# Layer 1's probabilities: transposed by VectorE and a DMA round trip in place of TensorE, with attention one slot later

## The chip, the cores and the metric

The kernel runs on one core of a Trainium2 chip. The core has TensorE (matrix products and transposes, into the eight banks of PSUM), VectorE, ScalarE, GpSimd and SyncE, which here only starts DMA transfers. In profile rows they are PE (PEld is its weight load), DVE, ACT, POOL and SP. Each engine runs its own instructions in order and waits for others through semaphores. The metric is the device time in microseconds. The kernel before takes 1692.25 us, the median of 3 runs (1692.12 to 1692.57).

## The reference, cut to what matters

Two layers, each a cross-attention and a feed-forward, are added to `x` (8 batches of 128 tokens, 512 wide). The change is in the attention of layer 1. It has 8 groups (one per key/value head), each of 4 query heads; queries and keys are normalised before the scores. Keys and values come from 128 context tokens and from the 128 tokens themselves, so a row has 256 keys.

```python
kv = jnp.concatenate([context, latents], axis=1)
q = rms_norm((latents @ Wq)...)          # 32 heads of 128
k = rms_norm((kv @ Wk)...)               # 8 heads of 128
v = (kv @ Wv)...
scores = jnp.einsum('bhgqd,bhkd->bhgqk', qg, k) * scale
probs = jax.nn.softmax(scores.astype(jnp.float32), axis=-1)
out = jnp.einsum('bhgqk,bhkd->bhgqd', probs, v)
return out @ Wo                          # 4096 -> 512
```

## The kernel before

Every product is made of three passes: each fp32 operand is split in a high part (rounded to fp32r) and a low part (the rest), and high x high, low x high and high x low are added in PSUM. ScalarE mostly makes the high parts and VectorE the low parts (`*_hi`, `*_lo`).

Layer 1 is 64 **slots**, 8 groups `t` of 8 batches `j`; slot `i = 8t + j`. The order of work is written out by hand for each engine in its `slot1(t, j)`; groups 1 to 6 are a hardware loop. Slot `i` works on several stages of different batches at once (counts start at 1, so head `i` is the one whose scores were made in slot `i - 1`):

- TensorE (`slot1` at L2498): keys and values of `i + 2`, transposes of queries and keys of `i + 1` (L2514, L2519), the output projection of `i - 1`, the transposes of the probabilities of `i` (L2488, eight 128x128 ones), the queries of `i + 2`, the scores of `i + 1`, the attention output of `i`.
- ScalarE (L1222): four exponentials of `i` (L1204), high parts of transposed queries (L1230) and keys (L1232), of the values with the squares of the keys (`kv_out`, L1182 and L1183), of the transposed probabilities (L1215), copy and squares of the queries (L1189, L1190), the high part of the attention output (L1220).
- VectorE (L1936): two reciprocals of the sums (L1917), low parts of queries and keys (L1945, L1947), in slots 1 to 5 of a group the low part of a piece of the next group's weights (`split_lo`, L1865), the addition of the projected output to the residual (L1921), low parts of the values (L1875), mean square of the keys (L1870), in slots 0 to 4 the high part of a weight piece (`split_hi`, L1859), the low part of the transposed probabilities (L1927), scaling of the keys (L1882), mean square of the queries (L1889, L1891), the maxima of the scores (L1907) and the shift of the exponentials `nb` (L1912), the low part of the attention output (L1933).
- GpSimd (L741): multiplies the probabilities by the reciprocals in two halves (L748), and two small powers (L610).
- SyncE (L566): one load of keys and values of the context per slot (L554) and one of weights in slots 1 to 5 (L577).

Each PSUM bank of layer 1 has one use: queries `Q1B`, scores `S0B` and `S1B`, transposed probabilities `T0B` and `T1B`, attention output `O1B`, projection `Y1B`.

Of the kernel before, what the change touches and what calls it, by code (L numbers as in the profile page):

```python
# [57 lines left out]
def build(nc, x, ctx_t, mask, gates, wk0, wv0, wq0, w0, bias0, lnw, qweight, lut4, lut8, ffn0_bias, w1, qk_norm, ffn1_w, ffn1_bias, out):  # L58
    stack = ExitStack()
    with stack:  # L60
# [184 lines left out]
        def z_rows(phase_no, b):  # L245
# [123 lines left out]
        kv1d = nc.dram_tensor("keys_values_of_context_of_layer_1", (KV, P, B, 256), fp32, kind="Internal").ap()  # L369


        @block.sync
        def _(sp):
# [192 lines left out]
            def slot1(t, j):  # L566
# [32 lines left out]
        def _(pool):  # L599
# [141 lines left out]
            def slot1(t, j, tail=False):  # L741
# [3 lines left out]
                if not (first and j == 0):  # L745
                    for half_p, done in ((0, norm1_first), (2, norm1_second)):
# [3 lines left out]
                                           ALU.mult).then_inc(done, 1)  # L750
# [29 lines left out]
        def _(act):  # L780
# [419 lines left out]
            def exponentials1(count, parity):  # L1200
                act.wait_ge(shift1_done, count)
                wait(act, pt1_ps, count - 1)
                for a in range(4):
# [3 lines left out]
                    if a == 1:  # L1207
                        last_op.then_inc(exp1_first, 1)
                last_op.then_inc(exp1_done, 1)

            def probabilities_hi(count):
                act.wait_ge(pt1_ps, count)
                wait(act, o1_ps, count - 1)
                for kc, done in ((0, pt1_hi_first), (1, pt1_hi_second)):
                    nc.scalar.activation(pt_hi[:, kc, :], (T0B, T1B)[kc][:, :], ACT.Copy).then_inc(done, 1)  # L1215

            def output1_hi(count):
                act.wait_ge(o1_ps, count)
                wait(act, y1_ps, count - 1)
                nc.scalar.activation(ot1_hi[:, :], O1B[:, :], ACT.Copy).then_inc(ot1_hi_done, 1)  # L1220

            def slot1(t, j):  # L1222
# [19 lines left out]
                if not (first and j == 0):  # L1242
# [8 lines left out]
                if not (first and j == 0):  # L1251
# [27 lines left out]
        def _(dve):  # L1279
# [650 lines left out]

            def output1_lo(count):
                dve.wait_ge(ot1_hi_done, count)
                nc.vector.tensor_tensor(ot1_lo[:, :], O1B[:, :], ot1_hi[:, :].bitcast(fp32),  # L1933
                                        ALU.subtract).then_inc(ot1_lo_done, 1)

            def slot1(t, j):  # L1936
# [20 lines left out]
                if last and j in (3, 5, 7):  # L1957
# [682 lines left out]
```

## Time and profile before

| | |
|---|---|
| median of 3 runs | 1692.25 us (1692.12 to 1692.57) |
| span of the profiled execution | 1690.2 us, of which layer 1's slots are about the last 750; its own time is given as this span alone |
| TensorE busy | 1669.2 us, 99% |
| VectorE busy | 1190.2 us, 70% |
| ScalarE busy | 1001.1 us, 59% |
| GpSimd busy | 601.3 us, 36% |
| chain that ended last | TensorE 87%, VectorE 7%, ScalarE 3% |
| granted TensorE clock | nine tenths of full speed or more in all 40 slices |

The runs' times are some 2 us above the span, which is from the first to the last instruction. The busy time of an engine counts overlapping instructions once. The chain that ended last is followed back from the last instruction, at each step to what released it or to the instruction before on its engine. An idle time in brackets in a row of the timeline is the time that the engine stood just before that instruction, with what released it.

### The profile page before, as it was taken

The page shows a single profiled execution, that of the slowest core. Times are in us where ns is not written, and L with a number is a line of the kernel's source. Part 1 is how long each engine was busy: PE and PEld are TensorE (multiplying, and loading weights), DVE is VectorE, ACT ScalarE, POOL GpSimd, SP SyncE. Part 2 cuts the span into 40 slices and gives each one's busy share as a digit, 9 for nine tenths or more (in the row PEclk, how much of TensorE's full clock was granted, in tenths as well). Part 3 has the DMA queues.
Part 4 walks back from the last instruction along what each step waited for, and adds up shares of the span by engine and source line. Part 5 has one row for each costly group of instructions (what it writes and reads, how often), then busy time and mean ns, then how long its engine had stood idle before and what let it go on. Part 6 is the DMA issues. An engine that isn't in the chain of part 4 may idle for free.

```text
span 1690.2 us, 30970 instructions
## 1 busy us (share of the span) xinstructions
PE 1669.2 (99%) x10269; PEld 1480.7 (88%) x10269; DVE 1190.2 (70%) x2245; ACT 1001.1 (59%) x2540; POOL 601.3 (36%) x584
## 2 busy tenths in 40 slices
PE   9999999999999999999999999999999999999998
PEld 8999999999988888888888888888888888888887
DVE  6444437676787777777779776767686767777677
ACT  5444343345767677776776666566656665666663
POOL 3322223211433443534425533333333333333343
PEclk9999999999999999999999999999999999999999
DMA  6444444545233333333332110101010111111001
GB/s 236 176 161 149 149 169 153 193 138 179 77 108 100 110 111 99 124 99 109 111 104 96 35 51 26 63 22 50 25 62 22 50 37 49 35 37 40 14 7 50
DMA packets 80591, 153.31 MB, mean 91 GB/s; under 512 B 6544, under 2 KB 58128, under 8 KB 76944
## 3 DMA queue, kind: packets, MB, share of 16 engines
q1 hardware_dynamic: 80528, 152.50, 26.9%
q8 instruction: 36, 0.59, 0.1%
q14 instruction: 27, 0.22, 0.0%
HBM read 108.43 MB, written 44.04 MB: 90 GB/s over the span
## 4 chain that ended last, share of the span: by engine, by line
PE 87%; DVE 7%; ACT 3%; issue 2%; DMA 0%; POOL 0%; DVEq 0%; SPq 0%; ACTq 0%
PE bank L2091 21%; PE bank L2038 15%; PE bank L2040 15%; PE bank L2039 14%; PE bank L2268 6%; PE bank L2488 3%; PE bank L2226 2%; PE bank L2304 2%; PE bank L2388 2%; PE bank L2514 2%; DVE wl L1538 1%; PE bank L2214 1%; DVE sc L1546 1%; DVE residual L1553 1%; DVE residual L1555 1%
## 5 line engine op out<-in xcount | busy, mean ns | idle before, releaser
L2038 PE MATMUL bank<-w_hi,xt_hi 128*128 (+2 forms) x512 | 178.6, 349 | 0.8 <-DVE qt_lo L1945 0.8
L748 POOL TENSOR_TENSOR p<-p,rn 128x512 f32<-128x512 f32 x128 | 133.1, 1041 | 120.9 <-DVE rn L1917 117.8
L2040 PE MATMUL bank<-w_hi,xt_lo 128*128 (+2 forms) x512 | 173.1, 338 | 0.0
L2039 PE MATMUL bank<-w_lo,xt_hi 128*128 (+2 forms) x512 | 171.8, 336 | 0.0
L691 POOL TENSOR_TENSOR pr<-pr,rn 128x512 f32<-128x512 f32 x64 | 67.5, 1055 | 291.4 <-DVE rn L1563 291.4
L1204 ACT ACTIVATE p<-bank,nb,q_r 128x256 f32<-128x256 f32 x256 | 141.0, 561 | 4.4 <-DVE nb L1912 1.9
L610 POOL TENSOR_TENSOR q_r<-q_ms,half 128x4 f32<-128x4 f32 x64 | 64.4, 1007 | 193.7 <-DVE q_ms L1891 193.7
L1049 ACT ACTIVATE pr<-sc,nmax 128x128 f32<-128x128 f32 x256 | 99.9, 391 | 39.9 <-DVE nmax L1548 39.5
L2038 PE MATMUL bank<-w0o_hi,ot_hi 128*128 128x512 f32 x256 | 105.5, 412 | 5.0 <-DVE residual L1555 4.5
L610 POOL TENSOR_TENSOR k_r<-k_ms,half 128x2 f32<-128x2 f32 x64 | 56.9, 888 | 147.8 <-DVE k_ms L1870 147.8
L2038 PE MATMUL bank<-w_hi,ot_hi 128*128 (+1 forms) x256 | 106.1, 415 | 1.3 <-DVE ot_lo L1933 1.3
L2038 PEld LDWEIGHTS bank<-w_hi,xt_hi 128*128 128x128 f32 x512 | 96.6, 189 | 11.9 <-DVE qt_lo L1945 1.0
L2040 PEld LDWEIGHTS bank<-w_hi,xt_lo 128*128 128x128 f32 x512 | 96.4, 188 | 11.6
L2039 PEld LDWEIGHTS bank<-w_lo,xt_hi 128*128 128x128 f32 x512 | 96.7, 189 | 10.7
L2091 PE MATMUL bank<-vw_hi,t_hi 128*128 128x256 f32 x368 | 104.1, 283 | 0.6 <-DVE vw_lo L1327 0.6
L2091 PE MATMUL bank<-vw_hi,t_lo 128*128 128x256 f32 x368 | 104.1, 283 | 0.0
L2091 PE MATMUL bank<-vw_lo,t_hi 128*128 128x256 f32 x368 | 104.1, 283 | 0.0
L1220 ACT ACTIVATE ot_hi<-bank 128x512 fp32r<-128x512 f32 x64 | 38.3, 598 | 109.5 <-PE bank L2040 109.5
L1189 ACT ACTIVATE q_sb<-bank 128x512 f32<-128x512 f32 x64 | 38.2, 597 | 106.3 <-PE bank L2040 106.3
L2040 PE MATMUL bank<-w_hi,ot_lo 128*128 (+1 forms) x256 | 100.4, 392 | 0.0
L2040 PE MATMUL bank<-w0o_hi,ot_lo 128*128 128x512 f32 x256 | 100.1, 391 | 0.0
L2039 PE MATMUL bank<-w0o_lo,ot_hi 128*128 128x512 f32 x256 | 99.9, 390 | 0.0
(293 smaller groups left out, 5603.6 us busy)
## 6 DMA issues: line engine op xcount, KB each, us to landing
stage<-w SPq DMA_DIRECT2D x35, 512.0 KB, 3.3
keys_of_layer<-kout SPq DMA_DIRECT2D x16, 1024.0 KB, 4.8
values_of_layer<-vout SPq DMA_DIRECT2D x16, 1024.0 KB, 5.2
kt<-keys_of_layer SPq DMA_DIRECT2D x64, 256.0 KB, 3.4
vs<-values_of_layer SPq DMA_DIRECT2D x64, 256.0 KB, 2.8
vraw<-wv SPq DMA_DIRECT2D x10, 1024.0 KB, 6.8
kraw<-wk SPq DMA_DIRECT2D x16, 512.0 KB, 5.6
stage0o<-w SPq DMA_DIRECT2D x16, 512.0 KB, 3.2
```

The source lines that it names most:

```text
L610: pool.tensor_tensor(dst, src, exponent, ALU.pow).then_inc(done, 1)
L691: pool.tensor_tensor(by4(pr), by4(pr), rn[:, :].unsqueeze(2).to_broadcast([P, 4, P]), ALU.mult).then_inc(norm_done, 1)
L748: pool.tensor_tensor(p1[:, half_p:half_p + 2, :], p1[:, half_p:half_p + 2, :], rn1[:, half_p:half_p + 2].unsqueeze(2).to_broadcast([P, 2, ...
L1049: last_op = nc.scalar.activation(by4(pr)[:, a, :], by4(sc)[:, a, :], ACT.Exp, bias=nmax[:, a:a + 1], accum_out=ssum[:, a:a + 1])
L1204: last_op = nc.scalar.activation(p1[:, a, :], by2((S0B, S1B)[a // 2][:, :])[:, a % 2, :], ACT.Exp, bias=nb1[:, a:a + 1], scale=q_r[:, pari ...
L1220: nc.scalar.activation(ot1_hi[:, :], O1B[:, :], ACT.Copy).then_inc(ot1_hi_done, 1)
L2038: nc.tensor.matmul(out_ap, l_hi, r_hi, start=(c == 0), stop=False)
L2039: nc.tensor.matmul(out_ap, l_hi, r_lo, start=False, stop=False)
L2040: op = nc.tensor.matmul(out_ap, l_lo, r_hi, start=False, stop=(c == n - 1))
L2091: op = nc.tensor.matmul(out_ap, l, r, start=start, stop=False, skip_group_check=True)
L2268: op = nc.tensor.matmul(bank[which][:, :], l[:, a, c, :], r[:, c, :], start=start, stop=False, skip_group_check=True)
L2488: op = nc.tensor.transpose(by4((T0B, T1B)[kc][:, :])[:, a, :], p1[:, a, tok(kc)], ident[:, :])
```

## The change

For heads 1 to 60 TensorE no longer transposes the probabilities. VectorE transposes them in blocks of 32x32 (`probabilities_in_blocks`, two instructions of 128x512), SyncE writes the blocks to DRAM (512 KB, one DMA) and, once that has landed, reads them back with four DMAs that put each block where the full transpose has it (512 KB in all). ScalarE makes the high part and VectorE the low part from this copy in SBUF, one instruction of 1024 columns each in place of two of 512. The copy of head `i` is used in slot `i + 1`, so its attention output, projection and addition to the residual all come one slot later. For heads 61 to 64 TensorE transposes as before; slot 61 makes the attention output and projection of head 60 and the attention output of head 61. In the last group the row statistics and normalisations of the feed-forward that follows move by a slot.

```diff
+            pblk = place.enter_context(nc.sbuf_tensor("probabilities_in_blocks", [P, 1024], fp32))
+            ptr1 = place.enter_context(nc.sbuf_tensor("probabilities_transposed", [P, 2, 1024], fp32))
...
+        pbd = nc.dram_tensor("blocks_of_probabilities", (4, P, 1024), fp32, kind="Internal").ap()
+        LAGGED = U - 4
+        lagged = lambda t, j: not (isinstance(t, int) and t == TL - 1 and j >= LAGGED % BODY + 1)
+        in_blocks = lambda ap: ap.rearrange("p (kb kc a q) -> p a kc kb q", kb=4, kc=2, a=4)
+        by_key_block = lambda ap: ap.rearrange("p (qb kc n) -> p kc qb n", qb=4, kc=2)
...
 # SyncE, at the end of each slot, behind its two loads
+                if lagged(t, j) and not (static and t == 0 and j < 1):
+                    probabilities_round_trip(BODY * t + j, j % 4)
+            def probabilities_round_trip(count, place):
+                sp.wait_ge(blocks1_done, 2 * count)
+                sp.dma_start(pbd[place, :, :], pblk[:, :]).then_inc(blocks1_out, 16)
+                sp.wait_ge(blocks1_out, 16 * count)
+                for kb in range(4):
+                    sp.dma_start(ptr1[32 * kb:32 * (kb + 1), place % 2, :].rearrange("k (qb n) -> k qb n", qb=4),
+                                 pbd[place, :, 256 * kb:256 * (kb + 1)].rearrange("(qb k) n -> k qb n", qb=4)).then_inc(ptr1_in, 16)
...
 # ScalarE: behind the high part of the keys, ahead of kv_out
+            def moved_probabilities_hi(count, parity):
+                act.wait_ge(ptr1_in, 64 * count)
+                wait(act, o1_ps, count - 1)
+                nc.scalar.activation(pt_hi[:, :, :].rearrange("p kc (qb n) -> p kc qb n", qb=4), by_key_block(ptr1[:, parity, :]),
+                                     ACT.Copy).then_inc(pt1_hi_done, 1)
...
+                if (lagged(t, j) or i == LAGGED + 1) and not (first and j < 2):
+                    moved_probabilities_hi(i - 1, (j - 1) % 2)
...
 # VectorE
+            def moved_probabilities_lo(count, parity):
+                dve.wait_ge(pt1_hi_done, count)
+                nc.vector.tensor_tensor(pt_lo[:, :, :].rearrange("p kc (qb n) -> p kc qb n", qb=4), by_key_block(ptr1[:, parity, :]),
+                                        pt_hi[:, :, :].bitcast(fp32).rearrange("p kc (qb n) -> p kc qb n", qb=4),
+                                        ALU.subtract).then_inc(pt1_lo_done, 1)
+            def probabilities_in_blocks(count):
+                wait(dve, blocks1_out, 16 * (count - 1))
+                for half_p in (0, 2):
+                    dve.wait_ge(norm1_done, 2 * count - 1 + half_p // 2)
+                    nc.vector.transpose(in_blocks(pblk[:, :])[:, half_p:half_p + 2],
+                                        p1[:, half_p:half_p + 2, :].rearrange("p a (kc kb q) -> p a kc kb q", kc=2, kb=4)).then_inc(blocks1_done, 1)
...
+                if (lagged(t, j) or i == LAGGED + 1) and not (first and j < 3):
+                    accumulate1(i - 2, (j - 3) % B)
+                if not lagged(t, j) and i > LAGGED + 1:
                     accumulate1(i - 1, (j - 2) % B)
+                if lagged(t, j) and not (first and j < 1):
+                    probabilities_in_blocks(i)
...
+                if lagged(t, j) and not (first and j < 2):
+                    output1_lo(i - 1)
...
 # TensorE
-                if not (first and j < 2):
-                    output_projection1(i - 1, own if j >= 2 else other)
+                if (lagged(t, j) or i == LAGGED + 1) and not (first and j < 3):
+                    output_projection1(i - 2, own if j >= 3 else other)
...
-                if not (first and j < 1):
...
+                if not lagged(t, j):
+                    if i > LAGGED + 1:
+                        output_projection1(i - 1, own)
                     transposed_probabilities1(i)
...
+                if lagged(t, j) and not (first and j < 2):
...
+                    attention_output1(i - 1, (j - 2) % 4)
+                if not lagged(t, j):
+                    if i == LAGGED + 1:
+                        output_projection1(i - 1, own)
                     attention_output1(i, (j - 1) % 4)
```

The middle of a VectorE slot with both weight splits (`j` = 3, group 0), before. `residual` is the addition of the projection, `stage` the staged weights, and `fbias` here holds the scaled keys:

```order
L1947 SCALAR_TENSOR_TENSOR kt_lo<-bank,kw,kt_hi 128x256 [waits kt1_hi_done]
L1865 TENSOR_TENSOR w_lo<-stage,w_hi 128x1024 [waits w1_hi_2]
L1921 SCALAR_TENSOR_TENSOR residual<-bank,tg,residual 128x512 [waits y1_ps]
L1875 TENSOR_TENSOR v_lo<-keys_values_of_context,v_hi 128x128 [waits k1_squared]
L1875 TENSOR_TENSOR v_lo<-bank,v_hi 128x128
L1870 TENSOR_SCALAR k_ms<-k_ss 128x2 [waits k1_squared]
L1859 TENSOR_SCALAR w_hi<-stage 128x1024 [waits w1_in_3]
L1927 TENSOR_TENSOR pt_lo<-bank,pt_hi 128x512 [waits pt1_hi_first]
L1927 TENSOR_TENSOR pt_lo<-bank,pt_hi 128x512 [waits pt1_hi_second]
L1882 TENSOR_SCALAR fbias<-keys_values_of_context,k_r 128x128 [waits k1_root_done]
```

The same stretch of the same slot in the changed kernel:

```order
L2007 SCALAR_TENSOR_TENSOR kt_lo<-bank,kw,kt_hi 128x256 [waits kt1_hi_done]
L1907 TENSOR_TENSOR w_lo<-stage,w_hi 128x1024 [waits w1_hi_2]
L1963 SCALAR_TENSOR_TENSOR residual<-bank,tg,residual 128x512 [waits y1_ps]
L1984 STREAM_TRANSPOSE probabilities_in_blocks<-p 128x2x2x4x32 [waits norm1_done,blocks1_out]
L1984 STREAM_TRANSPOSE probabilities_in_blocks<-p 128x2x2x4x32 [waits norm1_done]
L1917 TENSOR_TENSOR v_lo<-keys_values_of_context,v_hi 128x128 [waits k1_squared]
L1917 TENSOR_TENSOR v_lo<-bank,v_hi 128x128
L1912 TENSOR_SCALAR k_ms<-k_ss 128x2 [waits k1_squared]
L1901 TENSOR_SCALAR w_hi<-stage 128x1024 [waits w1_in_3]
L1975 TENSOR_TENSOR pt_lo<-probabilities_transposed,pt_hi 128x1024 [waits pt1_hi_done]
L1924 TENSOR_SCALAR fbias<-keys_values_of_context,k_r 128x128 [waits k1_root_done]
```

Two transposes have come in ahead of the values' low parts, and the two low parts of the probabilities from PSUM have become one from SBUF at the same place.

TensorE between the output projection (`w_hi,ot_hi`) and the queries (`w_hi,xt_hi`), group 0, before:

```order
L2038 MATMUL bank<-w_hi,ot_hi 128x512
L2039 MATMUL bank<-w_lo,ot_hi 128x512
L2040 MATMUL bank<-w_hi,ot_lo 128x512
L2488 MATMUL bank<-ident,p 128x128 [waits norm1_first,pt1_lo_done]
L2488 MATMUL bank<-ident,p 128x128 x3
L2488 MATMUL bank<-ident,p 128x128 [waits norm1_second]
L2488 MATMUL bank<-ident,p 128x128 x3
L2038 MATMUL bank<-w_hi,xt_hi 128x512 [waits qt1_lo_done]
```

And in the changed kernel, same place:

```order
L2113 MATMUL bank<-w_hi,ot_hi 128x512
L2114 MATMUL bank<-w_lo,ot_hi 128x512
L2115 MATMUL bank<-w_hi,ot_lo 128x512
L2113 MATMUL bank<-w_hi,xt_hi 128x512 [waits qt1_lo_done]
L2114 MATMUL bank<-w_lo,xt_hi 128x512
```

The eight transposes are gone from between them.

## Rows read from the trace of the kernel before

**Rows 1.** The page's first part: busy time of each engine.
```profile
PE 1669.2 (99%) x10269; PEld 1480.7 (88%) x10269; DVE 1190.2 (70%) x2245; ACT 1001.1 (59%) x2540; POOL 601.3 (36%) x584
```

**Rows 2.** Busy time by window: slot 2 of group 5 (columns PE, PEld, DVE, ACT, POOL, clock, DMA).
```profile
1417.84:1429.12 11.28, 11.28 (x69) 9.96 (x69) 8.84 (x20) 6.94 (x22) 4.16 (x5) 1.00 0.16 58
```

**Rows 3.** TensorE's waits, 1010 to 1690 us: total, times, longest.
```profile
PE bank L2038 <- DVE ot_lo L1933: 1.3, 3, 0.8
```

**Rows 4.** The chain that ended last, 1485 to 1690 us: start, duration.
```profile
1498.15 0.87 PE bank L2488 x8
```

**Rows 5.** Timeline of VectorE, the same slot 2: start, duration, line, operation.
```profile
1417.84 0.69 DVE L1945 TENSOR_TENSOR qt_lo<-bank,qt_hi 128x512 fp32r<-128x512 f32 x1 [0.32 <-ACT qt_hi L1230]
...
1418.84 1.22 DVE L1865 TENSOR_TENSOR w_lo<-stage,w_hi 128x1024 f32 x1
1419.98 0.74 DVE L1921 SCALAR_TENSOR_TENSOR residual<-bank,tg,residual 128x512 f32<-128x512 f32 x1
...
1421.11 0.69 DVE L1859 TENSOR_SCALAR w_hi<-stage 128x1024 f32 x1
1421.71 1.28 DVE L1927 TENSOR_TENSOR pt_lo<-bank,pt_hi 128x512 fp32r<-128x512 f32 x2
1422.91 0.28 DVE L1882 TENSOR_SCALAR fbias<-keys_values_of_context,k_r 128x128 f32<-128x128 f32 x1
...
1423.99 0.69 DVE L1889 TENSOR_REDUCE q_ss<-q_sq 128x4 f32<-128x512 f32 x1 [0.55 <-ACT q_sq L1190]
...
1426.11 0.16 DVE L1912 TENSOR_TENSOR nb<-nmax,q_r 128x4 f32<-128x4 f32 x1
...
1429.12 0.69 DVE L1945 TENSOR_TENSOR qt_lo<-bank,qt_hi 128x512 fp32r<-128x512 f32 x1 [0.32 <-ACT qt_hi L1230]
```

**Rows 6.** Timeline of ScalarE, in and around the same slot.
```profile
1419.35 0.20 ACT L1183 ACTIVATION_READ_ACCUMULATOR fbias<-bank 128x1 f32 x1
1420.10 1.09 ACT L1215 ACTIVATE pt_hi<-bank 128x512 fp32r<-128x512 f32 x2 [0.55 <-PE bank L2488]
...
1426.31 0.56 ACT L1204 ACTIVATE p<-bank,nb,q_r 128x256 f32<-128x256 f32 x1
...
1428.49 0.60 ACT L1230 ACTIVATE qt_hi<-bank 128x512 fp32r<-128x512 f32 x1
...
1429.32 0.33 ACT L1182 ACTIVATE v_hi<-keys_values_of_context 128x128 fp32r<-128x128 f32 x1
```

**Rows 7.** Timeline of VectorE in slot 6, which has no weight split: all its waits.
```profile
1464.35 0.75 DVE L1921 SCALAR_TENSOR_TENSOR residual<-bank,tg,residual 128x512 f32<-128x512 f32 x1 [0.30 <-PE bank L2040]
...
1465.85 1.29 DVE L1927 TENSOR_TENSOR pt_lo<-bank,pt_hi 128x512 fp32r<-128x512 f32 x2 [0.28 <-ACT pt_hi L1215]
...
1469.11 0.69 DVE L1889 TENSOR_REDUCE q_ss<-q_sq 128x4 f32<-128x512 f32 x1 [1.52 <-ACT q_sq L1190]
```

**Rows 8.** Groups by line, 1194 to 1284 us: busy us, mean ns.
```profile
L1907 DVE TENSOR_REDUCE nmax<-bank 128x2 f32<-128x512 f32 x16 | 10.3, 686 | 0.0
...
L1859 DVE TENSOR_SCALAR w_hi<-stage 128x1024 f32 x5 | 3.4, 685 | 0.0
```

**Rows 9.** DMA issues, whole run: KB each, median us to landing.
```profile
stage<-w SPq DMA_DIRECT2D x35, 512.0 KB, 3.3
...
keys_values_of_context<-lues_of_context_of_layer SPq DMA_DIRECT2D x64, 128.0 KB, 2.4
...
lues_of_context_of_layer<-kout SPq DMA_DIRECT2D x8, 512.0 KB, 4.0
```

**Rows 10.** Timeline of TensorE: two matmuls of 512 columns in one product.
```profile
1405.45 0.39 PE L2040 MATMUL bank<-w_hi,ot_lo 128*128 x1
...
1405.68 0.40 PE L2038 MATMUL bank<-w_hi,ot_hi 128*128 x1
```

**Rows 11.** Timeline of TensorE, first group: its first wait for probabilities.
```profile
954.40 0.63 PE L2488 MATMUL bank<-ident,p 128*128 128x128 f32 x4 [2.18 <-POOL p L748]
```

**Rows 12.** Timeline of VectorE in the last group.
```profile
1611.78 1.29 DVE L1294 BATCH_NORM_STATS2 stats<-residual 128x6 f32<-128x512 f32 x2
```

More of the change, by code:

```diff
@@ L749, in slot1 @@
                                            rn1[:, half_p:half_p + 2].unsqueeze(2).to_broadcast([P, 2, 256]),
-                                           ALU.mult).then_inc(done, 1)
+                                           ALU.mult).then_inc(norm1_done, 1)
+                if last and j == 6:
+                    row_roots(3, 1)
                 if not tail and not (last and j == BODY - 1):
@@ L1201, in exponentials1 @@
                 act.wait_ge(shift1_done, count)
-                wait(act, pt1_ps, count - 1)
+                if isinstance(count, int) and count > LAGGED + 1:
+                    act.wait_ge(pt1_ps, count - 1 - LAGGED)
+                else:
+                    wait(act, blocks1_done, 2 * (count - 1))
                 for a in range(4):
@@ L1250, in slot1 @@
                     transposed_hi(2, 5)
-                if not (first and j == 0):
+                if (lagged(t, j) or i == LAGGED + 1) and not (first and j < 2):
+                    output1_hi(i - 1)
+                if not lagged(t, j):
+                    if i == LAGGED + 1:
+                        probabilities_hi(i)
                     output1_hi(i)
@@ L1956, in slot1 @@
                     transposed_lo(3, 0)
-                if last and j in (3, 5, 7):
-                    dve.wait_ge(acc1_done, i - 1)
-                    row_stats(3, (j - 3) // 2)
+                if last and j in (4, 7):
+                    dve.wait_ge(acc1_done, i - 2 if j == 4 else i - 1)
+                    row_stats(3, (4, 5, 7).index(j))
                 if last and j == 2:
@@ L1969, in slot1 @@
                     k_mean(i + 2)
+                if last and j in (5, 6):
+                    normed_rows(3, 2 * j - 10)
+                    normed_rows(3, 2 * j - 9)
                 if first and j == 0:
@@ L1979, in slot1 @@
                     split_hi(t + 1, j, (t + 1) % 2)
-                if lag1 and not (last and j == BODY - 1):
+                if (lagged(t, j) or i == LAGGED + 1) and not (first and j < 2):
+                    moved_probabilities_lo(i - 1, (j - 1) % 2)
+                if not lagged(t, j) and LAGGED + 1 < i < U - 1:
                     probabilities_lo(i)
@@ L1984, in slot1 @@
                     q_mean(i + 2)
+                if i == LAGGED + 1 if isinstance(i, int) else False:
+                    output1_lo(i - 1)
+                    probabilities_lo(i)
                 maxima1(i + 1, j % 2)
+                if last and i == LAGGED + 1:
+                    accumulate1(i - 1, (j - 2) % B)
+                    dve.wait_ge(acc1_done, i - 1)
+                    row_stats(3, 1)
                 if first and j == 0:
@@ L2527, in slot1 @@
                     transpose_rows(2, 5 + 2 * j)
-                if not (first and j < 1):
-                    if first and j == 1:
-                        pe.wait_ge(xt_lo_done, 3 * B - 2)
+                if not lagged(t, j):
+                    if i > LAGGED + 1:
+                        output_projection1(i - 1, own)
                     transposed_probabilities1(i)
@@ L2539, in slot1 @@
                     pe.wait_ge(facc_done, B)
+                if not lagged(t, j) and i == LAGGED + 1:
+                    attention_output1(i - 1, (j - 2) % 4)
                 pe.wait_ge(qt1_lo_done, i + 1)
                 pe.wait_ge(kt1_lo_done, i + 1)
-                wait(pe, exp1_done, i)
+                wait(pe, exp1_done, 2 * i)
                 for a in range(4):
@@ L2546, in slot1 @@
                 op.then_inc(s1_ps, 1)
[L2547 to L2548 removed]
+                if lagged(t, j) and not (first and j < 2):
+                    if first and j == 2:
                         pe.wait_ge(xt_lo_done, 3 * B)
+                    attention_output1(i - 1, (j - 2) % 4)
+                if not lagged(t, j):
+                    if i == LAGGED + 1:
+                        output_projection1(i - 1, own)
                     attention_output1(i, (j - 1) % 4)
```

78 lines of the change are left out of this document (41 added, 37 removed).

## The prediction

> **What bounds the kernel now.** I read the page first: TensorE is busy for 99% of the span, VectorE for 70% [rows 1]. A busy TensorE is not yet a bound one, so the waits came next: from 1010 us to the end TensorE waits for named work 1.3 us in three places [rows 3], and the chain that ended last runs through each slot's eight transposes as a piece of 0.87 us [rows 4]. In layer 1 the pace is TensorE's: 11.28 us a slot, in which VectorE is busy 8.84 us [rows 2]. Taking 0.87 us out of TensorE gives a pace of 10.41 us, if nothing else needs longer.
>
> VectorE's timeline says something else does. VectorE's work is a ring through ScalarE: it issues `nb`, ScalarE runs four exponentials and the high part of the queries, and only then can VectorE start `qt_lo`; all its other work but `ot_lo` and two reciprocals stands behind that. From `nb` at 1426.11 to the next `qt_lo` at 1429.12 are 3.01 us [rows 5], of which ScalarE is in the exponentials and the copy from 1426.31 on [rows 6]. Once around is 11.28 us (1417.84 to 1429.12), and the one real wait in it, outside those 3.01 us, is 0.55 us before `q_ss` [rows 5]. So in a slot with both weight splits the ring alone needs 10.73 us. It is 0.55 us off the bound while its engine shows as 78% busy. Without `w_lo` (1.14 us from its start to the next one's, 1418.84 to 1419.98) it needs 9.59, without `w_hi` (0.60 us) 10.13 [rows 5]; with neither, 11.28 less three waits of 0.30, 0.28 and 1.52 leaves 9.2 us, or 9.0 by subtracting the steps [rows 5, 7]. I use 9.1.
>
> **The change, part by part.**
>
> TensorE: 60 of 64 transposes of heads go, 60 x 0.87 = 52 us [rows 4]. That is the most the change can give.
>
> VectorE, probabilities in blocks: two instructions of 512 columns from SBUF, which no row shows. Bounds: VectorE has two speeds here: 1024 columns take a step of 0.60 us in `w_hi` and of 1.14 us in `w_lo` [rows 5]. At the fast one 512 columns would take about 0.34; at half the slow one they would take what 1024 take in `w_lo`, 1.14 us. Between them stand the rows of 512 columns: 0.60 us a step for `pt_lo` (1.20 us for two [rows 5]), and 0.686 us for the maxima, 0.66 as a step [rows 8]. I take the middle of these two, 0.63 each, 1.26 for both; the bounds of the pair are 0.68 and 2.28 us.
>
> The Trainium skill ("Vector Engine (DVE) Microarchitecture Reference", 3.8 The reshape front-end and per-opcode configuration) has the transpose sustain one element per cycle and lane, and end with a step that only drains leftover reads. That speaks for the slow speed with a little on top, as taken. "VectorE: DVE Perf Modes", The three transpose paths, gives 311 ns for 128 columns in bf16; no row here shows a transpose on VectorE.
>
> VectorE, the low part of the probabilities: one instruction of 1024 columns from SBUF like `w_lo`, a step of 1.14 in place of 1.20 us [rows 5]: 0.06 less. The addition to the residual and `ot_lo` keep their place and size.
>
> The ring therefore grows by 1.26 - 0.06 = 1.20 us in every slot, and nothing hides it. The blocks wait for the second normalisation by GpSimd, which is done before VectorE comes to them, so they cost their own time and no wait. Against TensorE's 10.41:
>
> - slots 1 to 4 of a group: 10.73 + 1.20 = 11.93
> - slot 0: 9.59 + 1.20 = 10.79
> - slot 5: 10.13 + 1.20 = 11.33
> - slots 6 and 7: 9.1 + 1.2 = 10.3, so TensorE's 10.41
>
> A group of eight takes 4 x 11.93 + 10.79 + 11.33 + 2 x 10.41 = 90.66 us, against 8 x 11.28 = 90.24: 0.42 us longer. Of the 7 us that TensorE gets back per group, none arrives. For groups 1 to 6: +2.5 us.
>
> The first group differs. Before, TensorE stood 2.18 us for the first head's probabilities [rows 11]; the slot of that wait becomes some 1.1 us shorter, slots 0 and 2 stay, 3 and 4 cost 0.65 each, 5 costs 0.05, 6 and 7 give 0.87 each: -1.5 us. The last group has no weight splits: four slots give 0.6 to 0.87 us each, -2.9 in all. Slot 4 of it has the ring (10.3) with the pair of statistics (1.29 us [rows 12], some 1.7 with what follows them) and a copy of ScalarE: about 12.4, +1.1. Slot 61 carries the deferred attention output and projection, 6 + 12 matmuls of 512 columns at 0.23 us (1405.45 to 1405.68 [rows 10]) = 4.1 us, with the transposes back: +4.1, of which the slots around it, disturbed before, give back about 0.9. The last group: +1.4 us.
>
> ScalarE: the high part is one instruction of 1024 columns where two took 1.09 us [rows 6]; no change in its work. But it now stands ahead of `kv_out`. Counted from `qt_lo` (1417.84, next 1429.12), `kv_out` ran from 0.20 to 1.71 [rows 6]; with 1.09 ahead it ends at 2.8, and VectorE comes to the low parts of the values behind the blocks at 3.0 (no `w_lo`) or 4.1. It costs nothing by 0.2 us, as long as the data are there.
>
> SyncE and the DMA: the round trip of head i starts when its blocks are done and must have landed when ScalarE wants it in the next slot. The same arithmetic gives the time allowed: the slot's length less 2.6 us (1.09 + 1.51), plus or minus 1.14 where only one of the two slots has `w_lo`: 9.3 us for slots 1 to 5, 7.6 to 7.8 for slots 6, 7 and 0. The trip: a write of 512 KB, 3.3 us as a load or 4.0 as a write took [rows 9], then four reads of 128 KB. Issued close together they should take what one load of 512 KB takes, 3.3 us, to 4.0; one by one they would take 4 x 2.4 = 9.6 [rows 9]. That is 6.6 to 8.0 us, 13.6 at the far end. I take 7.3, no cost, since they wait for one another in nothing; 8.0 would cost 0.3 us in 25 slots. In SyncE's queue the next loads of context stand behind the trip; they are wanted a slot and more later.
>
> The sum: +2.5 - 1.5 + 1.4 = +2.4 us on the span of 1690.2, 1692.6. The runs are 2.05 us above the span (1692.25), so 1694.7 us.
>
> **The rivals.**
>
> A. Not slower: the transposes run at the fast speed of `w_hi` [rows 5, 8]. For it: one source, SBUF to SBUF, fp32, like `w_hi`. Against: every other row of 512 columns is at the slow one. The pair costs 0.68; a group takes 4 x 11.35 + 10.41 + 10.75 + 20.82 = 87.4, -2.9 each, the first group -4.4, the last +0.3: 1671 us. It decides from 1.20 us for the pair downwards, where the sum reaches zero (0.1 us of the pair is 4.2 us of the time).
>
> B. The ring is not rigid and TensorE's 0.87 us arrives: -52 + 4 for slot 61, 1644 us. Against it: `nb`, exponentials, `qt_hi`, `qt_lo` are in order on both engines, with the same 3.01 us in every slot.
>
> C. The transposes are twice as long, 1.14 each. A group takes 98.6 (slots 6 and 7 bound by the ring too), +8.4 x 6, first group +5.4, last +6.2: 1754 us; at 0.85 each about 1713. Scaling the skill's 311 ns with the columns ("VectorE: DVE Perf Modes", The three transpose paths) would give an estimate of 1.24 us each, above this end.
>
> D. The round trip becomes the bound in the slots without `w_lo`. It shares the DMA with a weight load of 512 KB issued shortly before [rows 9]. At 8.7 us it costs 1.0 us in 25 slots: 1720 us. It decides from 7.7 us on.
>
> **How the numbers follow.** About 0.2% (3.4 us) is what a measurement tells from no change. The forecast 0.50: with 0.60 to 0.68 us a transpose and a trip under 8 us it lies between 1692 and 1701; 0.32 of it within 0.2%, 0.17 slower, 0.01 faster. A 0.09 and B 0.07, faster; C 0.16 and D 0.18, slower, but for 0.02 where a small excess stays within. Faster 0.17, same 0.34, slower 0.49. The range 1671 to 1722 leaves out B, half of A's spread and the longer half of C. The likeliest one's own range is 1692 to 1701.
>
> **What would show it.** Right: TensorE's busy share falls, with waits for `qt_lo` or `pt_lo` in slots 1 to 5; VectorE's wait before `q_ss` is gone there, and its period is 11.9 us in slots 1 to 4, 10.4 in 6 and 7; the two transposes take a step of 0.63 us each. ScalarE does not wait for the round trip. Wrong: a wait of ScalarE ahead of the 1024-column copy (D), transposes of 0.34 or 1.1 us (A, C), or a period of 10.41 in slots 1 to 4 (B).

## The result, and the profile after

The changed kernel takes 1707.1 us, the median of 4 runs (1705.8 to 1707.8), against 1692.4 for the kernel before on the same chip: a ratio of 1.0085, 95% interval 1.0070 to 1.0099. It is slower by 14.7 us, a little under one per cent. The forecast of 1694.7 was 12.4 us too low; the range held the time, the likeliest case's own range (1692 to 1701) did not. The profiled span grew from 1690.2 to 1705.3 us.

The first part of the page and the first line of its chain, after:

```profile
PE 1641.6 (96%) x9789; PEld 1431.8 (84%) x9789; DVE 1246.2 (73%) x2305; ACT 986.5 (58%) x2480; POOL 625.7 (37%) x584
...
PE 44%; DVE 28%; ACT 12%; issue 10%; POOL 3%; DMA 1%; DVEq 0%; ACTq 0%; SPq 0%; POOLq 0%
```

TensorE is busy for 96% where it was 99% [rows 1], and only 44% of the chain is its own, 87% before. Its waits, where there had been 1.3 us [rows 3] (what was waited for, total, times, longest):

```profile
PE bank L2113 <- DVE pt_lo L1975: 31.9, 33, 1.1
PE bank L2113 <- DVE ot_lo L1990: 1.9, 2, 1.6
```

Slot 2 of group 5, as [rows 2] and [rows 5] show it of before. By window, with the columns of rows 2, and below it slot 6 of the same group:

```profile
1426.18:1438.03 11.85, 10.71 (x62) 9.11 (x61) 9.78 (x22) 6.69 (x21) 4.16 (x5) 1.00 0.43 144
1473.64:1484.44 10.80, 10.80 (x62) 9.09 (x61) 8.13 (x20) 6.70 (x21) 4.70 (x5) 1.00 0.33 109
```

VectorE's timeline in slot 2:

```profile
1426.18 0.69 DVE L2005 TENSOR_TENSOR qt_lo<-bank,qt_hi 128x512 fp32r<-128x512 f32 x1 [0.32 <-ACT qt_hi L1266]
...
1428.97 1.29 DVE L1984 STREAM_TRANSPOSE probabilities_in_blocks<-p 128x512 f32<-128x512 f32 x2
1430.19 0.25 DVE L1917 TENSOR_TENSOR v_lo<-keys_values_of_context,v_hi 128x128 fp32r<-128x128 f32 x1
...
1431.22 1.22 DVE L1975 TENSOR_TENSOR pt_lo<-probabilities_transposed,pt_hi 128x1024 fp32r<-128x1024 f32 x1
...
1432.82 0.68 DVE L1931 TENSOR_REDUCE q_ss<-q_sq 128x4 f32<-128x512 f32 x1
...
1434.93 0.16 DVE L1954 TENSOR_TENSOR nb<-nmax,q_r 128x4 f32<-128x4 f32 x1
...
1438.03 0.69 DVE L2005 TENSOR_TENSOR qt_lo<-bank,qt_hi 128x512 fp32r<-128x512 f32 x1 [0.32 <-ACT qt_hi L1266]
```

The two transposes take a step of 1.22 us together (1428.97 to 1430.19), the wait before `q_ss` is gone, and from `nb` to `qt_lo` it is 3.10 us (3.01 before): a full ring of 11.85. TensorE is busy for 10.71 of it. So far this is the forecast. In slots 5, 6 and 7 VectorE has a wait that before did not have. First VectorE in slot 6 of after; then GpSimd in slots 5 and 6 of after; then GpSimd and VectorE in slot 5 of the kernel before:

```profile
1476.95 1.23 DVE L1975 TENSOR_TENSOR pt_lo<-probabilities_transposed,pt_hi 128x1024 fp32r<-128x1024 f32 x1
1478.77 0.29 DVE L1924 TENSOR_SCALAR fbias<-keys_values_of_context,k_r 128x128 f32<-128x128 f32 x1 [0.59 <-POOL k_r L631]
```

```profile
1466.33 1.60 POOL L631 TENSOR_TENSOR k_r<-k_ms,half 128x2 f32<-128x2 f32 x1 [3.82 <-DVE k_ms L1912]
...
1477.13 1.60 POOL L631 TENSOR_TENSOR k_r<-k_ms,half 128x2 f32<-128x2 f32 x1 [2.69 <-DVE k_ms L1912]
```

```profile
1455.12 0.70 POOL L610 TENSOR_TENSOR k_r<-k_ms,half 128x2 f32<-128x2 f32 x1 [2.63 <-DVE k_ms L1870]
1454.95 1.28 DVE L1927 TENSOR_TENSOR pt_lo<-bank,pt_hi 128x512 fp32r<-128x512 f32 x2
```

The power of two numbers a lane, `k_r`, started 0.17 us behind `pt_lo` in the kernel before and took 0.70 us. Now it starts at 1477.13, as close behind `pt_lo` (1476.95), takes 1.60 us and ends at 1478.73, 0.55 us after `pt_lo`. VectorE's next instruction needs it. The chain that ended last runs through it in each of these slots:

```profile
1477.13 1.61 POOL k_r L631
```

That TensorE shows as busy for all of the 10.80 us of slot 6 is no sign that it bounds the slot: hi_on_scalar_too below runs the same matmuls in 10.39. From 1010 us on VectorE's waits list `k_r` as

```profile
DVE fbias L1924 <- POOL k_r L631: 15.3, 26, 0.6
```

The DMA issues, after (KB each, median us to landing), with the two new ones:

```profile
blocks_of_probabilities<-probabilities_in_blocks SPq DMA_DIRECT2D x60, 512.0 KB, 2.9
probabilities_transposed<-blocks_of_probabilities SPq DMA_DIRECT2D x240, 128.0 KB, 2.8
stage<-w SPq DMA_DIRECT2D x35, 512.0 KB, 3.3
keys_values_of_context<-lues_of_context_of_layer SPq DMA_DIRECT2D x64, 128.0 KB, 2.7
```

The weight load takes what it took [rows 9]. ScalarE waits for the round trip in two places, 0.7 us in all:

```profile
ACT pt_hi L1241 <- DMA probabilities_transposed<-blocks_of_probabilities: 0.7, 2, 0.4
```

Slot lengths are read as the distance between two `qt_lo` in VectorE's timeline. They account for the 15.1 us of the span: 1.9 arise before layer 1; the first group is 91.19 against 90.35 (+0.84); groups 1 to 6 are 91.62 against 90.24 (+8.3); the last seven slots 83.71 against 79.86 (+3.85); 0.2 behind them.

### The profile page after: what moved, and what is told of

It is laid out like the page before. It is cut to its first block, busy times and chain, and to the rows that moved or that the text cites. A ratio compares the mean times of both kernels' runs of the same rounds, so it can differ in the third digit from the quotient of the medians.

```text
span 1705.3 us, 30574 instructions
## 1 busy us (share of the span) xinstructions
PE 1641.6 (96%) x9789; PEld 1431.8 (84%) x9789; DVE 1246.2 (73%) x2305; ACT 986.5 (58%) x2480; POOL 625.7 (37%) x584
## 4 chain that ended last, share of the span: by engine, by line
PE 44%; DVE 28%; ACT 12%; issue 10%; POOL 3%; DMA 1%; DVEq 0%; ACTq 0%; SPq 0%; POOLq 0%
PE bank L2166 20%; ACT p L1232 7%; PE bank L2343 6%; DVE probabilities_in_blocks L1984 4%; PE bank L2113 4%; PE bank L2115 3%; PE bank L2114 3%; DVE nmax L1949 3%; POOL k_r L631 2%; DVE q_ss L1931 2%; DVE pt_lo L1975 2%; PE bank L2301 2%; PE bank L2379 2%; DVE qt_lo L2005 2%; ACT qt_hi L1266 2%
## 5 line engine op out<-in xcount | busy, mean ns | idle before, releaser
L631 POOL TENSOR_TENSOR k_r<-k_ms,half 128x2 f32<-128x2 f32 x64 | 80.8, 1263 | 205.8 <-DVE k_ms L1912 205.8
L2115 PEld LDWEIGHTS bank<-w_hi,xt_lo 128*128 128x128 f32 x512 | 97.0, 189 | 11.4
L2114 PEld LDWEIGHTS bank<-w_lo,xt_hi 128*128 128x128 f32 x512 | 97.4, 190 | 10.9
L2114 PE MATMUL bank<-w_lo,ot_hi 128*128 (+1 forms) x256 | 100.1, 391 | 0.0
```

What stands on the lines that cost most here:

```text
L631: pool.tensor_tensor(dst, src, exponent, ALU.pow).then_inc(done, 1)
L2114: nc.tensor.matmul(out_ap, l_hi, r_lo, start=False, stop=False)
L2115: op = nc.tensor.matmul(out_ap, l_lo, r_hi, start=False, stop=(c == n - 1))
```

## The experiments

They ran in three sets, each on a chip of its own: `e1` to `e4`; then `lo_on_gpsimd_mean_first_load_later`, `hi_on_scalar_too`, `e5` and `e6`; then `lo_on_gpsimd_load_later`, `pt_lo_in_halves` and `before_three_moves`. The kernel before took 1692.9, 1693.6 and 1693.1 us beside them.

**e1_blocks_added.** The kernel before plus the two transposes of VectorE, whose result nobody reads:

```diff
+ for half_p, ready in ((0, norm1_first), (2, norm1_second)):
+     dve.wait_ge(ready, i)
+     nc.vector.transpose(pblk...[:, half_p:half_p + 2], p1[:, half_p:half_p + 2, :]...)
```

> The kernel before, with the two block transposes of heads 1 to 60 added on VectorE behind the addition to the residual; nothing reads their result, TensorE still transposes. Theory (the ring of VectorE and ScalarE is 0.55 us short of TensorE's pace in slots 1 to 4): these slots go from 11.28 to about 11.9 us, slot 5 to 11.35, the others stay, 2.6 us a group: 1710 us. Rival (VectorE has 30% of its time free, so 1.2 us a slot are hidden): 1692 us, no change. Second rival (it is the DMA round trip that costs the changed kernel its time): also no change here.

Measured 1706.5 us, ratio 1.0081 (1.0064 to 1.0097). Slots 1 to 4 went from 11.28 to 11.83; slots 5 and 6 came to 11.22 and 11.0, the rest stayed (group 92.1). So 0.55 us of a pair of 1.22 were paid and 0.67 were free. That is more than the wait of 0.55 us in front of `q_ss`, because an instruction that does not wait starts while the one before it still shows as busy. The end of `fbias` and `q_ss`, before and in e1:

```profile
1423.10 0.34 DVE L1882 TENSOR_SCALAR fbias<-bank,k_r 128x128 f32<-128x128 f32 x1
1423.99 0.69 DVE L1889 TENSOR_REDUCE q_ss<-q_sq 128x4 f32<-128x512 f32 x1 [0.55 <-ACT q_sq L1190]
```

```profile
1433.62 0.35 DVE L1883 TENSOR_SCALAR fbias<-bank,k_r 128x128 f32<-128x128 f32 x1
1433.88 0.68 DVE L1890 TENSOR_REDUCE q_ss<-q_sq 128x4 f32<-128x512 f32 x1
```

From start to start it is 0.89 us before and 0.26 here: 0.63 us of room, and 0.03 more come from shorter steps of `v_lo` and `k_ms`. The ring needed 10.6 us, not 10.73.

**e2_blocks_left_out.** The changed kernel with the transposes cut to 32 columns, so that most of the probabilities it moves are stale.

```diff
- nc.vector.transpose(in_blocks(pblk)[:, half_p:half_p + 2], p1[:, half_p:half_p + 2, :]...)
+ nc.vector.transpose(pblk[:, 32 * half_p:32 * half_p + 32], p1[:, half_p, 0:32])
```

> The changed kernel with the block transposes cut to 32 columns each from head 2 on, so the probabilities that come back from DRAM are mostly stale; round trip, copies and everything else as in the changed kernel. Theory: the ring loses about 1.1 us a slot, so slots 1 to 4 need 10.7, slot 5 and 6 and 7 run near TensorE's 10.4 to 10.8: about 85 us a group in place of 91.6, 1707 - 6.5 x 7 = 1661 us. Rival (round trip or contention of its DMA traffic): stays near 1705.

Measured 1671.3 us (0.9874, 0.9857 to 0.9890), 10 above the expectation. Slots 1 to 4 were 10.84 and more. Two things were left: `k_r`'s wait of 0.59 us stayed, and now ScalarE did wait for the round trip, because the write took longer (with the shorter transposes it goes out 0.7 us behind the weight load, and the reads follow 4.5 us after it):

```profile
1425.05 1.07 ACT L1241 ACTIVATE pt_hi<-probabilities_transposed 128x1024 fp32r<-128x1024 f32 x1 [0.81 <-DMA probabilities_transposed<-blocks_of_probabilities]
...
blocks_of_probabilities<-probabilities_in_blocks SPq DMA_DIRECT2D x60, 512.0 KB, 3.9
```

**e3_mean_first.** The changed kernel with two calls of VectorE swapped, so that GpSimd gets the input of `k_r` 0.4 us earlier, before `pt_lo` starts.

```diff
-     v_low(i + 2, (j + 1) % 4)
      k_mean(i + 2)
+     v_low(i + 2, (j + 1) % 4)
```

> The changed kernel with the mean square of the keys ahead of the low parts of the values, so GpSimd can start its power 0.37 us earlier. Slots 5 to 7 wait 0.59 us for that power. Theory A (GpSimd cannot finish while VectorE runs the 1024-column subtraction of two SBUF operands, and ends 0.55 us after it): no change, 1707 within 2 us, the power only gets longer, 1.60 to about 2 us. Theory B (the power simply takes 1.6 us from its start): 0.37 us less in 3 slots of a group, 7 us in all, 1700 us.

Measured 1694.3 us, ratio to before 1.0010 (1.0000 to 1.0019): 12.8 us off the changed kernel by an exchange of neighbours. Both expectations were too high; neither theory had it that `k_r` is not held up at all once it starts first. VectorE and GpSimd in slot 6:

```profile
1467.81 0.13 DVE L1912 TENSOR_SCALAR k_ms<-k_ss 128x2 f32<-128x2 f32 x1
...
1468.25 1.22 DVE L1975 TENSOR_TENSOR pt_lo<-probabilities_transposed,pt_hi 128x1024 fp32r<-128x1024 f32 x1
1469.38 0.28 DVE L1924 TENSOR_SCALAR fbias<-keys_values_of_context,k_r 128x128 f32<-128x128 f32 x1
```

```profile
1468.02 0.70 POOL L631 TENSOR_TENSOR k_r<-k_ms,half 128x2 f32<-128x2 f32 x1 [2.29 <-DVE k_ms L1912]
```

Started 0.2 us ahead of `pt_lo`, `k_r` takes 0.70 us although `pt_lo` runs over most of it. Slots 5, 6, 7 fell from 11.92, 10.79, 10.79 to 11.24, 10.15, 10.43; slot 0 rose from 10.73 to 11.00; slots 1 to 4 stayed at 11.85.

**e4_split_on_gpsimd.** The changed kernel with `split_lo` (`w_lo`, 1.14 us of the ring in slots 1 to 5) moved to GpSimd behind the normalisations.

```diff
  # pool's slot1, ahead of k_root (taken out of dve's slot1)
+ if not last and 1 <= j < 6:
+     split_lo(t + 1, j - 1, (t + 1) % 2)
```

> The changed kernel with the low part of the next group's weights (w_lo, 1.14 us on VectorE in slots 1 to 5) made by GpSimd, behind its two normalisations. Theory (the ring bounds): slots 1 to 5 shrink by 1.1 us, to 10.7 to 10.8; 5.6 us a group, 39 in all: 1668 us, faster than the kernel before. GpSimd's 2.4 us for it (as in the first weights) delay its power for the keys, which could give back up to 0.5 us a slot (1685). Rival (TensorE or the DMA bounds): 1707, unchanged.

Measured 1700.3 us (1.0044, 1.0029 to 1.0058), where up to 1685 stood. Slots 1 and 3 fell to 10.9, slots 2 and 4 were 11.7 to 12.4, and slot 6, 10.79 in the changed kernel, was up to 12.2. GpSimd and VectorE in slot 1 of group 5, SyncE's issues and, below, ScalarE in slot 2:

```profile
1411.69 2.42 POOL L765 TENSOR_TENSOR w_lo<-stage,w_hi 128x1024 f32 x1
1412.60 1.29 DVE L1992 STREAM_TRANSPOSE probabilities_in_blocks<-p 128x512 f32<-128x512 f32 x2
```

```profile
1414.29 0.36 SPq L587 DMA_DIRECT2D stage<-w  x1
1414.76 0.36 SPq L594 DMA_DIRECT2D blocks_of_probabilities<-probabilities_in_blocks  x1
1419.71 1.76 SPq L597 DMA_DIRECT2D probabilities_transposed<-blocks_of_probabilities  x4
```

```profile
1424.02 1.06 ACT L1249 ACTIVATE pt_hi<-probabilities_transposed 128x1024 fp32r<-128x1024 f32 x1 [1.85 <-DMA probabilities_transposed<-blocks_of_probabilities]
```

The weight load waits for `w_lo` and stands ahead of the blocks' write in SyncE's order. The blocks are ready at 1413.89, but `w_lo` ends on GpSimd only at 1414.11: the load goes out at 1414.29 and the write 0.47 us behind it, 0.87 us after the blocks were ready (in the changed kernel it goes out at once). Then the reads wait for the write: 4.95 us here, 3.12 in the changed kernel (there the load is 1.73 us ahead), 2.65 with no load ahead. So the trip is longer by both, the hold in the queue and the slower write. This is rival D, called up by a relief elsewhere.

**lo_on_gpsimd_mean_first_load_later.** Both moves, and on SyncE the load behind the round trip:

```diff
-     if piece is not None: ...stage load...
      if lagged(t, j) and not (static and t == 0 and j < 1):
          probabilities_round_trip(BODY * t + j, j % 4)
+     if piece is not None: ...stage load...
```

> The changed kernel with three moves: k_mean ahead of v_low on VectorE (as in e3_mean_first), split_lo on GpSimd (as in e4_split_on_gpsimd), and the stage load issued behind the round trip on SyncE's queue instead of ahead of it. Theory: e4_split_on_gpsimd gained only in every other slot because the 512 KB stage load was issued 0.47 us ahead of the blocks' write, whose landing then took 4.95 us (1414.76 to 1419.71) where it took 3.12 in the changed kernel; with the load behind, slots 1 to 4 are all near 10.9 us, slots 5, 6, 7 and 0 as in e3_mean_first (11.24, 10.15, 10.43, 11.00): a group of 86.4 against 90.2, so 1667 us. Rival A, the write is slow whatever stands ahead of it (GpSimd's and the DMA's traffic in general): slots 2 and 4 stay at 12.2 and the time is near 1684. Rival B, the stage load now comes too late for split_hi: VectorE waits for stage and slots 1 to 4 rise above 11.85, time over 1694.

Measured 1663.5 us, ratio 0.9825 (0.9808 to 0.9841). The group is 85.6: slots 1 to 4 10.9, then 10.3, 10.3, 10.4 and 11.0.

**hi_on_scalar_too.** That kernel with `w_hi` made by ScalarE:

```diff
  # act's slot1, between q_out and output1_hi (taken out of dve's slot1)
+ if not last and j < 5:
+     wait(act, y1_ps if j >= 3 else q1_ps, 8 * t)
+     split_hi(t + 1, j, (t + 1) % 2)      # nc.scalar.activation(..., ACT.Copy)
```

> lo_on_gpsimd_mean_first_load_later with split_hi moved from VectorE to ScalarE as well, between q_out and output1_hi, where ScalarE waits 2.2 us for TensorE. Theory: VectorE loses another 0.6 us in slots 1 to 4 and is no longer what they wait for; TensorE sets all slots at its own 10.2 to 10.4 us: a group of 83.0 and 1645 us. Rival A, the round trip binds first (its 7.6 us need a slot of about 10.3 us, and more beside the stage load): slots of 10.7 to 11, 1660 to 1668. Rival B, ScalarE's copy of 1.0 us pushes output1_hi and so output1_lo and the exponentials: slots no shorter than without it, 1667 or more.

Measured 1649.2 us, ratio 0.9746 (0.9729 to 0.9762): the fastest of all, 43 us below the kernel before by the ratio (44 by the medians). The page's first part, and slot 2 of a group by window:

```profile
PE 1617.0 (98%) x9789; PEld 1431.6 (87%) x9789; DVE 1195.9 (73%) x2235; ACT 1021.1 (62%) x2515; POOL 674.4 (41%) x619
```

```profile
1383.37:1393.76 10.39, 10.39 (x62) 9.14 (x61) 8.23 (x20) 7.64 (x22) 6.16 (x6) 1.00 0.50 164
```

Nearly every slot of groups 1 to 6 is 10.39 us, TensorE busy throughout: the pace of 10.41 that the prediction derived as 11.28 - 0.87. Neither rival came: the round trip fits slots of 10.39, and ScalarE had the time.

**e5_before_lo_on_gpsimd** and **before_three_moves.** The controls: the kernel before with the same `split_lo` on GpSimd, and with all three moves of engine and order.

> The kernel before with split_lo on GpSimd alone. It is the control for the two runs above: the kernel before is bound by TensorE at 11.28 us a slot, so 1.1 us less on VectorE buys nothing: 1692, no change. Rival, VectorE's 0.55 us of slack is what hides other delays, or the subtraction of 2.4 us on GpSimd delays p and TensorE's transposes of it: 1700 or more.

> The kernel before with what made the changed kernel fast: k_mean ahead of v_low, split_lo on GpSimd, split_hi on ScalarE. Theory: TensorE's 11.28 us a slot stays the bound, so no change: 1692 us; the 43 us of hi_on_scalar_too then come from the change itself, freed by the moves. Rival, the moves are worth something without the change too: under 1688. Rival, ScalarE has less room here, since pt_hi comes late in its slot, and the copy delays output1_hi: over 1697.

Measured 1693.4 (1.0001, 0.9991 to 1.0010) and 1692.7 us (0.9997, 0.9988 to 1.0006); the group is 90.24 in the second, to the hundredth that of the kernel before. The moves alone are worth nothing. The change alone costs 14.7 us. Together they give 43.

**e6_blocks_written_twice.** The changed kernel, the write of the blocks done twice, one waiting for the other.

```diff
  sp.dma_start(pbd[place, :, :], pblk[:, :]).then_inc(blocks1_out, 16)
+ sp.wait_ge(blocks1_out, 32 * count - 16)
+ sp.dma_start(pbd[place, :, :], pblk[:, :]).then_inc(blocks1_out, 16)
```

> The changed kernel with the write of the blocks to DRAM done twice, one after the other: the round trip is one write and its landing longer, 7.6 + 3.0 = 10.6 us. Theory: in the changed kernel the trip has 0.6 us to spare in slots of 10.8 us (8.2 allowed) and 1.7 in slots of 11.85 (9.3 allowed), so with 3 us more all slots become 13.2 us: a group of 105.6 against 91.6, 1812 us. Rival, the trip has spare of several us because something else absorbs it (the second buffer of ptr1): no change, 1707. If the trip already bound the changed kernel, the whole 3 us would show in every slot: 64 x 3 = 190, 1897 us.

Measured 1738.7 us (1.0265, 1.0246 to 1.0285): the trip does bind with a second write of 2.65 us in it, but at a third of the expected price. (In the slots with a weight load it grew by some 2.2 us, since the two writes took 5.3 us together for the 3.1 of the one behind the load.) ScalarE's wait in slot 0 of a group:

```profile
1426.42 1.06 ACT L1243 ACTIVATE pt_hi<-probabilities_transposed 128x1024 fp32r<-128x1024 f32 x1 [1.42 <-DMA probabilities_transposed<-blocks_of_probabilities]
```

The slots of group 4 are 12.30, 11.85, 12.14, 11.92, 12.04, 11.92, 12.56 and 10.79: long and short in turn. The reason can be read from VectorE's order: in a slot the blocks come ahead of `pt_lo`, so a late trip delays `pt_lo` and the next slot's blocks, not this one's. By this reading that loop goes round once in two slots, and an excess is paid once in two. Slots 2, 4 and 6 of e4 show the same pattern. It was not tested apart.

**lo_on_gpsimd_load_later.** e4 with the load behind the round trip, and nothing else.

> e4_split_on_gpsimd with one edit more: the stage load is issued behind the round trip on SyncE's queue. It tells whether the load ahead of the blocks' write was what lengthened slots 2 and 4 there. Theory: the write of 512 KB lands after 2.7 us instead of 4.95, ScalarE waits no longer for probabilities_transposed, slots 1 to 4 are all 10.9 us and slots 5, 6, 7 and 0 stay at 10.8 because k_r beside pt_lo is as in the changed kernel: a group of 86.8 and 1673 us against 1700. Rival, k_mean ahead of v_low was the part that mended it in lo_on_gpsimd_mean_first_load_later: no change, 1700.

Measured 1675.7 us (0.9896, 0.9881 to 0.9911). Slots 1 to 4 are 10.9 each, and the median of the write fell:

```profile
blocks_of_probabilities<-probabilities_in_blocks SPq DMA_DIRECT2D x60, 512.0 KB, 2.6
...
stage<-w SPq DMA_DIRECT2D x35, 512.0 KB, 4.3
```

In e4 it was 4.9, with 4.2 for `stage`. The place in the queue alone is worth 24.6 us here. The edit takes away both the hold of 0.87 us and the slower write; what each is worth was not told apart.

**pt_lo_in_halves.** The changed kernel, `pt_lo` as two instructions of 512 columns.

```diff
- nc.vector.tensor_tensor(pt_lo[:, :, :]..., by_key_block(ptr1[:, parity, :]), pt_hi..., ALU.subtract)
+ for kc in range(2):
+     nc.vector.tensor_tensor(pt_lo[:, kc, :]..., by_key_block(ptr1[:, parity, :])[:, kc], pt_hi[:, kc, :]..., ALU.subtract)
```

> The changed kernel with pt_lo computed by two instructions of 512 elements instead of one of 1024, both still with two operands in SBUF. In the changed kernel k_r on GpSimd takes 1.60 us beside this instruction (0.70 alone) and ends 0.55 us behind it. Theory A, GpSimd is held up for as long as one such instruction runs and gets on between two: k_r ends about 0.6 us earlier, VectorE's wait of 0.59 us goes, less 0.06 us for the second instruction: slots 5, 6, 7 and 0 fall from 10.8 to 10.3, about 1696 us. Theory B, GpSimd is held up while any of them runs: k_r stays at 1.6 us and the time at 1707 or 3 us above it.

Measured 1698.2 us, ratio to before 1.0028 (1.0017 to 1.0038): 8.9 us below the changed kernel. GpSimd and VectorE in slot 5:

```profile
1461.22 1.07 POOL L631 TENSOR_TENSOR k_r<-k_ms,half 128x2 f32<-128x2 f32 x1 [3.82 <-DVE k_ms L1912]
```

```profile
1461.05 1.29 DVE L1976 TENSOR_TENSOR pt_lo<-probabilities_transposed,pt_hi 128x512 fp32r<-128x512 f32 x2
1462.33 0.29 DVE L1924 TENSOR_SCALAR fbias<-keys_values_of_context,k_r 128x128 f32<-128x128 f32 x1
```

`k_r` ends at 1462.29, about 0.6 us after the first half, and no longer holds up `fbias`. Theory A had it, with 1696 us. Slots 1 to 4 rose to 11.92 and slot 0 to 10.93; slots 5, 6 and 7 fell to 11.39, 10.26 and 10.5. More work on VectorE, and less time.

## Why the prediction was right and wrong

**What bounds, and where the gain went: right.** The prediction read the ring as needing 10.73 us of 11.28. e1 shows that it bounds, and that it needed 10.6: 0.67 us of a pair of 1.22 was free, the rest was paid. In the changed kernel 0.09 us came back between `nb` and `qt_lo` (3.10 for the 3.01 taken as fixed), hence 11.85 for 11.93; two small errors of opposite sign. And hi_on_scalar_too shows the other side: with VectorE relieved, TensorE's 0.87 us a slot arrives. Rival B fell in the kernel as changed.

**The price of the transposes: right.** 1.22 us for the pair against 1.26; rivals A (0.68) and C (2.28) fell.

**The slots.** Groups 1 to 6, against the prediction:

| slot | predicted | measured | with `k_mean` first (e3) |
|---|---|---|---|
| 0 | 10.79 | 10.73 | 11.00 |
| 1 to 4 | 11.93 | 11.85 | 11.85 |
| 5 | 11.33 | 11.92 | 11.24 |
| 6, 7 | 10.41 | 10.79 | 10.15, 10.43 |
| group | 90.66 | 91.62 | 90.21 |

**The failed step** is "The low part of the probabilities: one instruction of 1024 columns from SBUF like `w_lo`... 0.06 less". Its own time was right (a step of 1.13). What it does to GpSimd was not in the sum. Before, `pt_lo` read one operand from PSUM, and `k_r`, started 0.17 us behind it, took 0.70 us. e1 has the large transposes and keeps that form, and `k_r` takes 0.70 us as close behind it:

```profile
1467.28 0.70 POOL L611 TENSOR_TENSOR k_r<-k_ms,half 128x2 f32<-128x2 f32 x1 [3.82 <-DVE k_ms L1871]
1467.11 1.28 DVE L1928 TENSOR_TENSOR pt_lo<-bank,pt_hi 128x512 fp32r<-128x512 f32 x2
```

e2 has the new form without the large transposes, and `k_r` takes 1.60 in slots 5 to 7. So it is the form of `pt_lo`, not the transposes. In pt_lo_in_halves it is two instructions of 512 columns as before, with only the operand in SBUF in place of PSUM: `k_r` takes 1.07 for 0.70. So the operand's place counts, and the length of one instruction (1.60 for 1.07) beside it. The two edits that only touch who starts first (e3) and how long one instruction lasts (halves) take the wait away. In slots 0 to 4 `w_hi` stands between `k_ms` and `pt_lo`; there `k_r` takes 1.07 us in both kernels, ends about 0.55 us after `w_hi`, and is through in time. Slots 5, 6 and 7 have nothing there, which is why the excess over the prediction is 0.59, 0.38 and 0.38: 1.35 us a group, less 0.38 that slots 0 to 4 came out shorter, 5.8 of the 12.4 us that the forecast was too low.

The Trainium skill has the rule ("SBUF — State Buffer", Who interferes with whom): a VectorE instruction with two inputs in SBUF contends with a GpSimd instruction that reads SBUF. By its "Summary: rules for kernel authors" the second one to issue blocks until the first is finished. The traces agree: behind `pt_lo` 1.60 us, ahead of it 0.70, behind a half of it 1.07, behind the form with one input in PSUM 0.70. The prediction weighed what a transpose costs and did not ask what the operand's move from PSUM to SBUF changes for the neighbour. e3, which removes the wait, took 1694.3 us against the forecast's 1694.7. That closeness is in part luck: its groups 1 to 6 are 2.8 us shorter than forecast, and the rest of the span is some 2.5 us longer. That the range of 1671 to 1722 held the measured time is owed to its width, which was drawn for other terms (the transposes and the trip).

**The first group: wrong by 2.3 us** (+0.84 for -1.5). Slot 5 (11.84 for 11.33) and 6 and 7 (10.72 and 10.79 for 10.41) have the same cause. Slot 2 does not: it took 12.63 us for 11.28. TensorE stood 3.58 us for `qt_lo`, and its clock was granted at 0.50 in the stretch behind, the level of 1.2 GHz (columns as in rows 2):

```profile
968.39 0.79 PE L2113 MATMUL bank<-w_hi,xt_hi 128*128 128x512 f32 x1 [3.58 <-DVE qt_lo L2005]
...
969.83 0.63 PE L2113 MATMUL bank<-w_hi,xt_hi 128*128 128x512 f32 x1
970.26 0.63 PE L2114 MATMUL bank<-w_lo,xt_hi 128*128 128x512 f32 x1
```

```profile
970.00:974.00 4.00, 4.00 (x12) 3.13 (x11) 3.71 (x9) 0.09 (x1) 1.07 (x1) 0.50 0.73 260
```

A matmul of 512 columns takes a step of 0.43 us there (969.83 to 970.26) and 0.23 at full clock [rows 10]. The prediction had no such term. Across the changed kernels the length of this slot follows the stretch at that level: in after, e2 and lo_on_gpsimd_load_later it lasts almost 7 us and the slot takes 12.6 to 12.8; in e3, e4, pt_lo_in_halves, lo_on_gpsimd_mean_first_load_later and hi_on_scalar_too it lasts about 3.4 us and the slot takes 11.4 to 11.6 (both worked out from the clock that the profile gives for stretches of 2 us). TensorE stands 3.2 to 3.6 us ahead of it in all eight. Why the stretch is longer in three of them is open.

**The last group: wrong by 2.4 us** (+3.85 for +1.4). Slots 60 and 61 were priced well (12.38 for 12.4; +4.3 for +4.1 us in slot 61), but the four slots ahead gave 2.3 us where 2.9 stood, since they have no weight splits and so `k_r`'s wait, and the slot behind 61 took 0.7 more where 0.9 were to be given back.

**The round trip: right for the kernel, its price wrong.** It costs nothing, as taken. The write was followed by the reads after 3.12 us, and ScalarE was released 4.3 us after the reads' first issue where it waited for them (1419.71 to 1424.02 in e4): 7.4 us, for 7.3 taken. Rival D's rule (each us over is paid in every slot) is wrong by what e6 shows.

**Open.** 1.9 us arise before layer 1. The first `qt_lo` came between 944.1 and 946.5 us in thirteen profiles, at 946.3 in before_three_moves and 944.5 in a changed kernel; nothing in the edits explains it, and with one profile each it was not settled.

## What to carry to other kernels

An engine 78% busy can be the next bound at once: close the ring through the engines it hands work to, and take only the waits outside the hand-over as room (counted from start to start, since the bracketed idle time is a little short). Then relieve that engine with the change, not before it: neither half was worth anything alone. When an operand moves from PSUM to SBUF, ask who shares the port; when a wait goes, ask which transfer is now issued together with which.

## What the runs showed of the hardware

- A 128x512 fp32 transpose of 32x32 blocks on VectorE, SBUF to SBUF, is 0.685 us, a step of 0.61; of 32 columns 0.184.
- GpSimd's 2-column power is 0.70 us when it starts first or close behind a VectorE subtraction with one operand in PSUM, and ends 0.55 to 0.6 us after one with both operands in SBUF behind which it starts. It also ends about 0.55 us after `w_hi` (1024 columns from SBUF to SBUF with one input, a step of 0.60 us), 1.07 us in all. Its 1024-column subtraction takes 2.41 us where VectorE takes 1.21.
- A DRAM write of 512 KB was followed by its dependent reads after 2.65 us alone, 3.1 with a 512 KB load issued 1.7 us ahead, 4.5 with one 0.7 us ahead (e2), 4.95 with one 0.5 us ahead.
